# Cross-attention and graph layers on one core: router logits and low-rank activations computed row by row, and the router moved on VectorE

## The chip, the core and the metric

One core of a Trainium2 chip runs the whole program in one launch. The metric is the device time of that launch in microseconds. TensorE multiplies into PSUM, VectorE and ScalarE read PSUM, GpSimd works in SBUF only, and SyncE issues most DMAs. Each engine takes its own instructions in program order; they meet only through semaphores.

## What is computed

For 4 batches of 256 rows of 512 values (cut to what matters):

```python
# lora_A is ctx_4096 seen as (4, 64, 512); the kernel sums its 4 parts first
logits = x @ router_W.T + router_b            # (b, s, 8)
w      = softmax(logits)
a_sum  = einsum('bsh,arh->bsr', x, lora_A)    # (b, s, 64)
x1     = nan_to_num(x + 0.5 * sum_n w_n * (a_sum @ lora_B[n].T))
# 32 heads of cross-attention over 64 context rows, residual, layer norm
points = layernorm(x1 + attention(x1, ctx) @ Wo.T + bo) * g + b
# two graph layers of four blocks each; neighbours are the 8 nearest of 512 columns of ctx
for 8 blocks: p = leaky(points); points += (W_i @ (p + sum over 8 neighbours of p)) / 9
```

The diff touches the first four lines only. `a_sum` and the logits come out of one product with a matrix of 64 + 8 = 72 columns, `a_router`.

## The kernel before

The work on TensorE is cut into *uses* of PSUM. PSUM holds four slots of 1024 fp32 columns, and `tile_order()` writes out the order of all uses by hand, as (kind, batch, part). Use number n goes to slot n mod 4. Before TensorE starts use n, `wait_read` makes it wait until the reader of use n-4 is done (the table `read_by` says which semaphore and count that is); readers wait with `wait_full`. Every engine walks through the same list and does its own part of each kind, so the list is also the order of work on ScalarE, VectorE, GpSimd and SyncE.

The list has an opening for batch 0 (square, distance 0, lora_a, router, distance 1, keys, mixed, update, values, query). Then, for b = 0 to 2 with n = b+1, the attention of batch b is interleaved with the low-rank update and the neighbours of batch n: rows b, adjacency b, lora_a n, scores b 0 and 1, square n, router n, scores b 2 and 3, distance n 0, mixed n, shift b, update n, weights b, and so on. Batch 3's attention is interleaved with the first graph blocks, and the other graph blocks run in loops over two slots for W and two for the neighbour sums.

What the router does, kind by kind:

- **lora_a**: TensorE multiplies `a_router` (stationary, 72 columns) with `x_in` (moving, 256 columns), 4 chunks, so the result has 72 rows and one column per query (L538). ScalarE copies it to `low` (L746).
- **router**: TensorE turns `low` into two tiles of 128 queries by 72 columns with two transposes (L558). VectorE first waits for `q_lo` of the batch before (GpSimd's L913, since `mix` lies where `q_full` lay), then adds the bias (`lg`, L1168), takes the maximum and subtracts it (`lgs`, L1171). ScalarE takes the exponential (`lge`, L764). VectorE sums, inverts and multiplies (`lgw`, L1175) and writes `mix`, the low-rank activations times each of the 8 weights (L1177, two instructions).
- **mixed**: TensorE transposes `mix` (8 transposes, L572). ScalarE makes the high part `mixT_hi` (L773), VectorE the low part `mixT_lo` (L1187).
- **update**: TensorE multiplies with `lora_B` in three partial products (L576); it needs `mixT_lo`. VectorE adds the result to x and clamps it to `x1`.

Around it: **scores** (2 matmuls of 512 columns each, L593) are read by VectorE's four maxima (`shift`, L1243). **square** starts with ScalarE's `xyz_sq` (L758) and ends with its copy into `xyz_n` (L760). **distance** (2 fp32 products of 512 columns, L565, each recorded as two instructions) needs `xyz_n`; its reader is `nearest` on VectorE (L1034 to L1039), for part 0 of batches 1 to 3 only behind the shift. **adjacency** ends with ScalarE's copy to `adj` (L858). **shift** transposes the maxima (L598); SyncE sends them to `q_stack` (L443), and **weights** waits for that. From the second batch on, SyncE sends the inverted sums of the batch before (`inv_out`, L1049, made by VectorE behind the shift) ahead of it. GpSimd makes the next batch's `k_blk_hi` (L906) once scores 3 is done.

Of the kernel before, what the change touches and what calls it, by code (L numbers as in the profile page):

```python
# [17 lines left out]
ACT = mybir.ActivationFunctionType  # L18
# [30 lines left out]
def tile_order():  # L49

    order = [("square", 0, 0), ("distance", 0, 0), ("lora_a", 0, 0), ("router", 0, 0), ("distance", 0, 1),
             ("keys", 0, 0), ("mixed", 0, 0), ("update", 0, 0), ("values", 0, 0), ("query", 0, 0)]
    for b in range(B - 1):
        n = b + 1
        order += [("rows", b, 0), ("adjacency", b, 0), ("lora_a", n, 0), ("scores", b, 0), ("scores", b, 1),
                  ("square", n, 0), ("router", n, 0), ("scores", b, 2), ("scores", b, 3), ("distance", n, 0),
                  ("mixed", n, 0), ("shift", b, 0), ("update", n, 0), ("weights", b, 0), ("weights", b, 1)]
        order += [("output", b - 1, 0)] * (b > 0)
        order += [("weights", b, 2), ("distance", n, 1), ("attend", b, 0), ("weights", b, 3), ("query", n, 0),
                  ("attend", b, 1)]  # L60

    b = B - 1
    order += [("rows", b, 0), ("adjacency", b, 0)] + [("scores", b, i) for i in range(4)]
    order += [("wp", 0, 0), ("shift", b, 0), ("wp", 1, 0), ("spread", 0, 0), ("output", b - 1, 0),
              ("weights", b, 0), ("weights", b, 1), ("weights", b, 2), ("attend", b, 0), ("weights", b, 3),
              ("attend", b, 1), ("wp", 2, 0), ("spread", 1, 0), ("output", b, 0), ("spread", 2, 0),
              ("wp", 0, 1), ("wp", 3, 0), ("spread", 0, 1), ("wp", 1, 1), ("spread", 3, 0), ("wp", 2, 1),
              ("spread", 1, 1), ("wp", 3, 1), ("spread", 2, 1), ("spread", 3, 1)]
    return order


def xattn_graph_kernel(nc, xT, ctx, ctxT, mask, maskT, fsideT, lora_BT, router_WT, router_b,
# [9 lines left out]
    with stack:  # L82
# [5 lines left out]
        def sem(name):  # L88
            return stack.enter_context(nc.semaphore(name))
# [10 lines left out]
        def fb(name, shape, dt=F32):  # L100
            return sb(name, shape, dt, front)
# [19 lines left out]
        mixT_hi = fb("mixT_hi", [P, KC, S], F32R)  # L121
        low = fb("low", [R + NE, S])
        a_router = fb("a_router", [P, KC, R + NE])
# [91 lines left out]
        a_ready = sem("a_ready")  # L215
        low_ready = sem("low_ready")
        lgs_ready = sem("lgs_ready")
# [73 lines left out]
        def wait_full(eng, *key):  # L291
# [5 lines left out]
        read_by = {  # L297
            "lora_a": (low_ready, lambda b, i: b + 1), "keys": (k_ready, lambda b, i: KC),
            "values": (v_ready, lambda b, i: 1), "square": (norm_ready, lambda b, i: b + 1),
            "router": (mix_ready, lambda b, i: ST * (b + 1)), "distance": (near_ready, lambda b, i: KC * b + 2 * i + 2),  # L300
            "mixed": (mixT_lo_ready, lambda b, i: b + 1), "update": (raw_ready, lambda b, i: b + 1),
# [173 lines left out]
        def _(pe):  # L475
# [50 lines left out]
            for key in order:  # L526
# [5 lines left out]
                if kind == "lora_a":  # L532
                    loaded(pe, f"x{b}")
                    if b == 0:
                        pe.wait_ge(a_ready, 1)
                        loaded(pe, "routerW")
                    for k in range(KC):
                        last = mm(ps[0:R + NE, 0:S], a_router[:, k, :], x_in[:, k, :], k == 0, k == KC - 1)  # L538
                elif kind == "keys":
# [11 lines left out]
                elif kind == "square":  # L551
                    pe.wait_ge(sq_ready, b + 1)
                    pe.wait_ge(dve_consts, 2)
                    last = mm(ps[0:V + 1, 0:H], half_neg[:], xyz_sq[:], True, True)
                elif kind == "router":
                    pe.wait_ge(low_ready, b + 1)
                    for t in range(ST):
                        last = pe.transpose(ps[:, t * P:t * P + R + NE], low[:, t * P:(t + 1) * P],  # L558
                                            ident[0:R + NE, 0:R + NE])
                elif kind == "distance":  # L560
# [112 lines left out]
        def _(act):  # L673
# [64 lines left out]
            for key in order:  # L738
                kind, b, i = key
                ps = slot(key)  # L740
                if kind == "lora_a":
                    if b >= 1:

                        wait_full(act, "router", b - 1, 0)
                    wait_full(act, *key)
                    act.activation(low[:], ps[0:R + NE, 0:S], ACT.Copy).then_inc(low_ready, 1)  # L746
                elif kind == "keys":
# [5 lines left out]
                elif kind == "square":  # L753
# [6 lines left out]
                    act.activation(xyz_n[V:V + 1, :], ps[V:V + 1, 0:H], ACT.Copy).then_inc(norm_ready, 1)  # L760
                elif kind == "router":

                    act.wait_ge(lgs_ready, b + 1)
                    act.activation(lge[:], lgs[:], ACT.Exp).then_inc(lge_ready, 1)  # L764
                    if b == 0:
                        loaded(act, "loraB")
                        act.activation(flat(loraB_hi), flat(loraB_raw), ACT.Copy).then_inc(loraB_hi_ready, 1)
                elif kind == "mixed":
# [111 lines left out]
        def _(pool):  # L880
# [43 lines left out]
            for key in order:  # L924
                kind, b, i = key
                if kind == "router" and b == 0:
                    pool.wait_ge(loraB_hi_ready, 1)
# [50 lines left out]
        def _(dve):  # L978
# [166 lines left out]
            for key in order:  # L1145
# [5 lines left out]
                if kind == "values":  # L1151
# [4 lines left out]
                       .then_inc(v_ready, 1)  # L1156
                elif kind == "router":
                    loaded(dve, "rb")
# [213 lines left out]
```

## Time and profile before

| what | value |
|---|---|
| median of 3 runs | 461.76 us (461.59 to 470.96) |
| span of the profiled execution | 462.6 us |
| TensorE busy | 407.9 us, 88% |
| VectorE busy | 289.6 us, 63% |
| ScalarE busy | 157.7 us, 34% |
| GpSimd busy | 139.4 us, 30% |

All times in the profile are us from the span's first instruction. The first 264 us hold the attention, the rest the graph blocks. PE is TensorE's matmuls, PEld its weight loads, DVE VectorE, ACT ScalarE, POOL GpSimd, SPq the queue of SyncE. In a row of the timeline, "idle before <-releaser" is the time in which the engine had nothing to do ahead of that row, and what ended it. All matmuls are issued by one helper at L477, so they are told apart by the names behind the line: out <- moving, stationary. An fp32 product is recorded as two matmul instructions with two weight loads, a transpose as one.

### The profile page before, as it was taken

What the parts mean: (1) busy time and instruction counts of PE and PEld (TensorE: products, weight loads), DVE (VectorE), ACT (ScalarE), POOL (GpSimd) and SP (SyncE); (2) the same over time, 40 slices, a digit from 0 to 9 for tenths busy, and PEclk for the clock granted to TensorE, in tenths of its full rate; (3) what the DMA queues carried; (4) which work ended last, traced back from release to release, by engine and by line L of the source; (5) the groups of instructions that cost most, each with busy time, mean ns of one, the idle gap of its engine ahead of it and who ended that gap; (6) DMA issues with size and microseconds to landing.
All of it is one profiled execution on the core that took longest, in us unless ns stands there. A gap on an engine that the chain in (4) does not pass through costs nothing.

```text
span 462.6 us, 5745 instructions
## 1 busy us (share of the span) xinstructions
PE 407.9 (88%) x2216; PEld 333.7 (72%) x2216; DVE 289.6 (63%) x327; ACT 157.7 (34%) x193; POOL 139.4 (30%) x94
## 2 busy tenths in 40 slices
PE   5979297997899779968777989999999999999996
PEld 1566275784858475847365678898898888898894
DVE  1859828647783678596438764665656665665633
ACT  2230042364217522753182243223332224233310
POOL 2344723016003900190001223434424342344400
PEclk9999688999799979998989989999999999999999
DMA  6910434028120912013400000000000000000012
GB/s 202 408 63 0 150 77 110 14 94 162 31 68 8 186 40 91 4 44 85 99 3 25 1 0 1 0 2 0 0 0 1 1 0 0 0 0 0 0 75 107
DMA packets 22568, 24.90 MB, mean 54 GB/s; under 512 B 5508, under 2 KB 16756, under 8 KB 22548
## 3 DMA queue, kind: packets, MB, share of 16 engines
q1 hardware_dynamic: 21524, 23.44, 17.8%
q0 software_dynamic: 576, 1.18, 1.2%
q8 instruction: 13, 0.21, 0.2%
q10 hardware_dynamic: 448, 0.01, 0.1%
q14 instruction: 7, 0.06, 0.0%
HBM read 14.69 MB, written 3.38 MB: 39 GB/s over the span
## 4 chain that ended last, share of the span: by engine, by line
PE 68%; DMA 7%; DVE 6%; issue 6%; ACT 5%; SPq 4%; POOL 3%; DVEq 0%; ACTq 0%; POOLq 0%
PE slot L477 67%; DMA q_stack<-shiftT 3%; SPq L353 3%; DMA inv_bounce<-inv_out 2%; DMA sums_bounce<-sums 1%; ACT probT L813 1%; DVE shift L1243 1%; POOL points L921 1%; DVE p_lo L1122 1%; ACT attT L853 1%; POOL q_lo L913 1%; ACT sums L851 1%; DMA xyz_n<-in_ctx 1%; SPq L412 1%; DVE mix L1177 1%
## 5 line engine op out<-in xcount | busy, mean ns | idle before, releaser
L913 POOL TENSOR_TENSOR p_lo<-p_full,p_hi 128x1024 fp32r<-128x1024 f32 x29 | 69.5, 2398 | 160.8 <-ACT p_hi L688 160.8
L688 ACT ACTIVATE p_hi<-p_full 128x1024 fp32r<-128x1024 f32 x32 | 33.9, 1060 | 129.0 <-DVE p_full L997 128.9
L1086 DVE TENSOR_TENSOR u_lo<-slot,u_hi 128x1024 fp32r<-128x1024 f32 x32 | 38.8, 1222 | 49.6 <-ACT u_hi L729 49.6
L477 PE MATMUL slot<-adj,u_hi 128*128 128x512 f32 x256 | 64.8, 395 | 0.2
L477 PE MATMUL slot<-adj,u_lo 128*128 128x512 f32 x256 | 63.3, 389 | 0.0
L477 PE MATMUL slot<-fs_hi,p_hi 128*128 (+1 forms) x256 | 52.9, 289 | 7.5 <-DVE p_lo L1122 6.1
L1093 DVE SCALAR_TENSOR_TENSOR points<-slot,points 128x1024 f32<-128x1024 f32 x32 | 39.2, 1224 | 30.2 <-PE slot L477 30.2
L477 PEld LDWEIGHTS slot<-adj,u_lo 128*128 128x128 f32 x256 | 48.1, 188 | 10.0
L477 PEld LDWEIGHTS slot<-adj,u_hi 128*128 128x128 f32 x256 | 46.5, 188 | 10.3 <-issue 1.6
L477 PE MATMUL slot<-fs_lo,p_hi 128*128 (+1 forms) x256 | 52.8, 289 | 0.0
L477 PE MATMUL slot<-fs_hi,p_lo 128*128 (+1 forms) x256 | 52.7, 288 | 0.0
L477 PEld LDWEIGHTS slot<-fs_hi,p_hi 128*128 128x128 f32 x256 | 42.5, 197 | 10.5 <-issue 8.8
L997 DVE SCALAR_TENSOR_TENSOR p_full<-points 128x1024 f32<-128x1024 f32 x32 | 46.2, 1445 | 2.7
L477 PEld LDWEIGHTS slot<-fs_lo,p_hi 128*128 128x128 f32 x256 | 41.1, 198 | 0.0
L477 PEld LDWEIGHTS slot<-fs_hi,p_lo 128*128 128x128 f32 x256 | 41.0, 197 | 0.0
L729 ACT ACTIVATE u_hi<-slot 128x1024 fp32r<-128x1024 f32 x32 | 32.5, 1015 | 21.1 <-PE slot L477 20.4
L477 PE MATMUL slot<-probT,v_blk 128*128 128x256 f32 x128 | 30.8, 394 | 3.9 <-ACT probT L813 3.9
L477 PEld LDWEIGHTS slot<-probT,v_blk 128*128 128x128 f32 x128 | 24.9, 198 | 9.3 <-issue 3.1
L813 ACT ACTIVATE probT<-slot,mask_col 128x1024 f32<-128x1024 f32 x16 | 17.4, 1111 | 41.4 <-PE slot L477 41.3
L477 PE MATMUL slot<-wo,attT 128*128 128x512 f32 x64 | 28.3, 595 | 2.6 <-issue 2.6
L920 POOL TENSOR_TENSOR points<-points,g_all 128x1024 f32<-128x1024 f32 x2 | 4.7, 2356 | 66.4 <-DVE points L1080 66.4
L477 PEld LDWEIGHTS slot<-wo,attT 128*128 128x128 f32 x64 | 11.8, 190 | 16.8 <-issue 16.8
(138 smaller groups left out, 586.8 us busy)
## 6 DMA issues: line engine op xcount, KB each, us to landing
q_stack<-q_hi SPq DMA_DIRECT2D x32, 128.0 KB, 3.6
x_in<-in_xT SPq DMA_DIRECT2D x4, 512.0 KB, 4.0
q_stack<-q_lo SPq DMA_DIRECT2D x16, 128.0 KB, 4.5
out_points<-points SPq DMA_DIRECT2D x4, 512.0 KB, 2.8
inv_sums<-inv_bounce SPq DMA_DIRECT2D x7, 256.0 KB
loraB_raw<-in_lora_BT SPq DMA_DIRECT2D x1, 1024.0 KB, 9.4
wk<-in_WkT SPq DMA_DIRECT2D x1, 1024.0 KB, 11.5
wq_raw<-in_WqT SPq DMA_DIRECT2D x1, 1024.0 KB, 10.5
```

The source lines that it names most:

```text
L353: eng.dma_start(q_stack[PART * part:PART * (part + 1), j::HC // 2, :].bitcast(F32), q[PART * j:PART * (j + 1)].bitcast(F32))\
L412: sp.dma_start(inv_sums[:, 2 * i:2 * i + 2].rearrange("p c s -> p (c s)"), back.rearrange("g h n -> (g h) n").unsqueeze(1).broadcast_to([H ...
L477: return pe.matmul(dst, lhsT, rhs, start=start, stop=stop, skip_group_check=True)
L688: act.activation(p_hi[:, b, :], p_full[:, half, :], ACT.Copy).then_inc(p_hi_ready, 1)
L729: act.activation(u_hi[:, half].rearrange("p m o -> p (m o)"), ps[:], ACT.Copy)\
L813: act.activation(probT[:, i % 2, :], ps[:], ACT.Exp, bias=mask_col[:, b:b + 1], scale=QK_SCALE).then_inc(prob_ready, 1)
L851: act.activation(sums[V:2 * V, :], ps[V:2 * V, :], ACT.Copy).then_inc(att_read, 1)
L913: pool.tensor_tensor(lo, full, hi.bitcast(F32), ALU.subtract).then_inc(ready, 1)
L920: link(pool.tensor_tensor(pts, pts, g_all[:].unsqueeze(1).broadcast_to([P, ST, H]), ALU.mult))
L997: dve.scalar_tensor_tensor(p_full[:, half, :], pts, SLOPE, pts, ALU.mult, ALU.max)\
L1086: dve.tensor_tensor(u_lo[:, half].rearrange("p m o -> p (m o)"), ps[:], u_hi[:, half].rearrange("p m o -> p (m o)").bitcast(F32), ALU.subt ...
L1093: dve.scalar_tensor_tensor(pts, ps[:], 1.0 / (TOPK + 1), pts, ALU.mult, ALU.add)\
```

## The change

- `lora_a` swaps the operands: the 128 queries of a tile are now the stationary side and `a_router` the moving one. The result already has queries on rows, in the layout that the transposes gave. For each of 2 tiles 4 chunks are summed: 8 products of 72 columns instead of 4 of 256.
- The copy to `low`, the tile `low`, its semaphore and the two transposes go, and so does the use `router` of PSUM. The list is four uses shorter, and the slot distances of the uses near the former `router` change with it. The reader of a `lora_a` use is now VectorE's `mix`.
- What VectorE, ScalarE and GpSimd did at `router` they now do at `lora_a`. In batches 1 to 3 that is ahead of scores 0 and 1 on VectorE, and ahead of `xyz_sq` of the same batch on ScalarE.

```diff
-    order = [("square", 0, 0), ("distance", 0, 0), ("lora_a", 0, 0), ("router", 0, 0), ("distance", 0, 1),
+    order = [("square", 0, 0), ("distance", 0, 0), ("lora_a", 0, 0), ("distance", 0, 1),
...
         order += [("rows", b, 0), ("adjacency", b, 0), ("lora_a", n, 0), ("scores", b, 0), ("scores", b, 1),
-                  ("square", n, 0), ("router", n, 0), ("scores", b, 2), ("scores", b, 3), ("distance", n, 0),
+                  ("square", n, 0), ("scores", b, 2), ("scores", b, 3), ("distance", n, 0),
...
-            "lora_a": (low_ready, lambda b, i: b + 1), "keys": (k_ready, lambda b, i: KC),
+            "lora_a": (mix_ready, lambda b, i: ST * (b + 1)), "keys": (k_ready, lambda b, i: KC),
...
-                    for k in range(KC):
-                        last = mm(ps[0:R + NE, 0:S], a_router[:, k, :], x_in[:, k, :], k == 0, k == KC - 1)
+                    for t in range(ST):
+                        for k in range(KC):
+                            last = mm(ps[:, t * P:t * P + R + NE], x_in[:, k, t * P:(t + 1) * P],
+                                      a_router[:, k, :], k == 0, k == KC - 1)
...
-                elif kind == "router":
-                    pe.wait_ge(low_ready, b + 1)
-                    for t in range(ST):
-                        last = pe.transpose(ps[:, t * P:t * P + R + NE], low[:, t * P:(t + 1) * P],
-                                            ident[0:R + NE, 0:R + NE])
...
                 if kind == "lora_a":
-                    if b >= 1:
-
-                        wait_full(act, "router", b - 1, 0)
-                    wait_full(act, *key)
-                    act.activation(low[:], ps[0:R + NE, 0:S], ACT.Copy).then_inc(low_ready, 1)
+
+                    act.wait_ge(lgs_ready, b + 1)
+                    act.activation(lge[:], lgs[:], ACT.Exp).then_inc(lge_ready, 1)
+                    if b == 0:
+                        loaded(act, "loraB")
+                        act.activation(flat(loraB_hi), flat(loraB_raw), ACT.Copy).then_inc(loraB_hi_ready, 1)
...
-                if kind == "router" and b == 0:
+                if kind == "lora_a" and b == 0:
...
-                elif kind == "router":
+                elif kind == "lora_a":
                     loaded(dve, "rb")
                     if b >= 1:
```

What follows that last line is unchanged: `dve.wait_ge(q_lo_ready, b)`, the wait for the slot, and the router's instructions.

## Rows read from the trace of the kernel before

**Rows 1.** The profile's page: the chain that ended last, its shares by line.

```profile
PE slot L477 67%; DMA q_stack<-shiftT 3%; SPq L353 3%; DMA inv_bounce<-inv_out 2%; DMA sums_bounce<-sums 1%; ACT probT L813 1%; DVE shift L1243 1%; POOL points L921 1%; DVE p_lo L1122 1%; ACT attT L853 1%; POOL q_lo L913 1%; ACT sums L851 1%; DMA xyz_n<-in_ctx 1%; SPq L412 1%; DVE mix L1177 1%
```

**Rows 2.** The same chain in order of time: start, us, what.

```profile
268.50 63.48 PE slot L477 x384
```

**Rows 3.** Timeline, the opening: start us, us, instructions [idle before <-releaser].

```profile
11.26 3.62 PE L477 MATMUL slot<-x_in,a_router 128*72 128x256 f32 x8
...
15.35 0.50 PE L558 MATMUL slot<-ident,low 72*128 72x72 f32 x2 [0.47 <-ACT low L746]
15.64 3.71 PE L477 MATMUL slot<-xyz_n,xyz 65*128 65x512 f32 x4
...
19.15 9.01 PE L477 MATMUL slot<-ctx_t,wk 128*128 128x256 f32 x32
```

**Rows 4.** Timeline, stretch 1 (batch 1's router in batch 0's attention).

```profile
64.80 1.90 PE L477 MATMUL slot<-x_in,a_router 128*72 128x256 f32 x8
...
66.03 2.38 POOL L913 TENSOR_TENSOR q_lo<-q_full,q_hi 128x1024 fp32r<-128x1024 f32 x1 [10.69 <-ACT q_hi L791]
...
67.20 2.36 DVE L1243 TENSOR_REDUCE shift<-slot 128x16 f32<-128x1024 f32 x2 [1.80 <-PE slot L477]
...
69.57 0.34 PE L558 MATMUL slot<-ident,low 72*128 72x72 f32 x2
...
70.05 0.17 DVE L1168 TENSOR_TENSOR lg<-slot,rb_all 128x16 f32<-128x16 f32 x1 [0.50 <-PE slot L558]
...
70.67 0.22 ACT L764 ACTIVATE lge<-lgs 128x16 f32<-128x16 f32 x1 [0.41 <-DVE lgs L1171]
...
70.73 1.88 PE L477 MATMUL slot<-xyz_n,xyz 65*128 65x512 f32 x4
...
72.08 1.29 DVE L1177 TENSOR_TENSOR mix<-slot,lgw 128x512 f32<-128x512 f32 x2
...
73.52 1.07 PE L572 MATMUL slot<-ident,mix 128*128 128x128 f32 x8 [0.91 <-DVE mix L1177]
```

**Rows 5.** Single lines: duration ns min/median/max, first and last start us, forms.

```profile
L558 PE MATMUL slot<-ident,low x8: 226/282/382, 15.3 to 156.0; 72*128 72x72 f32 x8
...
L572 PE MATMUL slot<-ident,mix x8: 272/273/302, 73.5 to 74.3; 128*128 128x128 f32 x8
...
L1175 DVE TENSOR_TENSOR lgw<-lge,small x4: 175/720/817, 17.2 to 158.6; 128x16 f32<-128x16 f32 x4
```

**Rows 6.** Timeline, stretch 2 (batch 2's router in batch 1's attention).

```profile
105.06 1.88 ACT L858 ACTIVATE adj<-slot 128x2048 fp32r<-128x2048 bf16 x1
...
112.74 1.06 PE L572 MATMUL slot<-ident,mix 128*128 128x128 f32 x8 [0.91 <-DVE mix L1177]
...
116.66 0.55 DVE L1049 RECIPROCAL inv_out<-sums_in 64x64 f32<-64x64 f32 x1
...
125.45 1.19 PE L477 MATMUL slot<-q_stack,k_stack 100*128 100x256 f32 x8 [0.66 <-DMA q_stack<-shiftT]
```

**Rows 7.** Timeline, stretch 3 (batch 3's router in batch 2's attention).

```profile
152.20 1.88 ACT L858 ACTIVATE adj<-slot 128x2048 fp32r<-128x2048 bf16 x1
...
156.64 1.28 ACT L764 ACT_TABLE_LOAD   x1
...
160.87 1.06 PE L572 MATMUL slot<-ident,mix 128*128 128x128 f32 x8 [1.91 <-DVE mix L1177]
...
162.03 1.02 ACT L773 ACTIVATE mixT_hi<-slot 128x1024 fp32r<-128x1024 f32 x1 [3.88 <-PE slot L572]
...
163.53 1.23 DVE L1187 TENSOR_TENSOR mixT_lo<-slot,mixT_hi 128x1024 fp32r<-128x1024 f32 x1 [0.54 <-DMA sums_bounce<-sums]
...
165.48 0.55 DVE L1049 RECIPROCAL inv_out<-sums_in 64x64 f32<-64x64 f32 x1 [0.28 <-DMA sums_in<-sums_bounce]
```

**Rows 8.** Windows: us, PE, PEld, DVE, ACT, POOL busy, PEclk, DMA share, GB/s.

```profile
67.00:77.00 10.00, 6.08 (x25) 2.92 (x23) 8.72 (x14) 4.11 (x9) 5.45 (x5) 1.00 0.69 159
78.00:81.00 3.00, 3.00 (x16) 3.00 (x16) 2.90 (x7) 0.00 (x0) 0.00 (x0) 0.50 0.08 22
```

More of the change, by code:

```diff
@@ L121, in xattn_graph_kernel @@
         mixT_hi = fb("mixT_hi", [P, KC, S], F32R)
-        low = fb("low", [R + NE, S])
         a_router = fb("a_router", [P, KC, R + NE])
@@ L215, in xattn_graph_kernel @@
         a_ready = sem("a_ready")
-        low_ready = sem("low_ready")
         lgs_ready = sem("lgs_ready")
@@ L297, in xattn_graph_kernel @@
         read_by = {
-            "lora_a": (low_ready, lambda b, i: b + 1), "keys": (k_ready, lambda b, i: KC),
+            "lora_a": (mix_ready, lambda b, i: ST * (b + 1)), "keys": (k_ready, lambda b, i: KC),
             "values": (v_ready, lambda b, i: 1), "square": (norm_ready, lambda b, i: b + 1),
-            "router": (mix_ready, lambda b, i: ST * (b + 1)), "distance": (near_ready, lambda b, i: KC * b + 2 * i + 2),
+            "distance": (near_ready, lambda b, i: KC * b + 2 * i + 2),
             "mixed": (mixT_lo_ready, lambda b, i: b + 1), "update": (raw_ready, lambda b, i: b + 1),
@@ L760, in _ @@
                     act.activation(xyz_n[V:V + 1, :], ps[V:V + 1, 0:H], ACT.Copy).then_inc(norm_ready, 1)
-                elif kind == "router":
[L763 to L767, printed above, removed]
                 elif kind == "mixed":
@@ L1156, in _ @@
                        .then_inc(v_ready, 1)
-                elif kind == "router":
+                elif kind == "lora_a":
                     loaded(dve, "rb")
```

## The prediction

> **What bounds the kernel now.** I read the chain of waits first. By line, TensorE's helper holds two thirds of it and no single wait holds more than 3% [rows 1]. From 268.5 us on the chain in order of time is one row of matmuls after another (the first is shown) [rows 2], none of them touched by the change, so whatever the change does happens before that, where the chain changes engine every few microseconds. The timeline of those stretches shows four places: the opening (batch 0's router), and the three places where batch n's router runs inside batch n-1's attention; I call these stretch 1, 2 and 3, after n.
>
> In the opening TensorE is busy nearly without a break from 11.3 to 28.2 us and waits 0.47 us for `low` [rows 3]. In stretch 1 (64 to 79 us) the chain is: maxima, router, `mix`, the `mixed` transposes, `mixT_hi`, `mixT_lo`, `update`. TensorE is busy 6.1 of 10 us there, VectorE 8.7 [rows 8]: VectorE and its order set the pace, and TensorE waits 0.91 us for `mix` before L572 [rows 4]. In stretch 2 the same order holds, and behind `mixT_lo` come the reciprocal of the sums and, in SyncE's order, three DMAs; the `weights` matmuls wait 0.66 us for the last, the shift stack [rows 6]. In stretch 3 `mixT_lo` and the reciprocal themselves wait a little for DMAs (0.54 and 0.28 us) [rows 7].
>
> **The change, part by part.**
>
> *1. The lora_a matmuls.* Before: 4 fp32 products of 256 columns, each two instructions, so 8: 3.62 us in the opening [rows 3], 1.90 us in stretch 1 [rows 4]. The same eight instructions are 0.43 and 0.21 us apart, 4 and 2 cycles of 2.4 GHz per column, so the opening runs at the 1.2 GHz level although the clock records there say nothing. Now: 2 x 4 products of 72 columns, so 16 instructions of 72 columns on 128-column weights. No row has this form. The nearest are the two transposes of L558: 128 columns of weights, 72 moving, fp32. Two take 0.34 us where one takes 0.28, so they stand 0.06 us apart [rows 4, 5], and 0.50 against 0.38, 0.12 apart, at the low clock [rows 3, 5]. From above I bound them by the fp32 transposes with 128 columns moving, L572: eight take 1.07 us where one takes 0.27, so 0.11 apart [rows 4, 5]; 0.21 at the low clock. So 16 cost 0.96 to 1.8 us at the high clock and 1.9 to 3.4 us in the opening. Only two in a row were seen at 0.06, so I go by the middle. The Trainium skill, "TensorE: Matmul & The Clock Gate", section "LDWEIGHTS (loading the stationary operand)", says that a weight load costs its number of columns divided by 1.2, in ns, whatever the rows: 107 ns here. The two transposes 0.06 us apart don't agree, if what they show holds for more than two. By the rule the opening's 16 would take 1.9 us, since the low clock's spacing is already above 0.107, and the sum below would come out 0.4 us lower; in stretches 1 to 3 it changes nothing, because those matmuls end before what gates the router.
>
> *2. The copy and the transposes.* ScalarE's `low` (between the adjacency copy and `xyz_sq`) and two transposes go. In stretches 1 to 3 both lie beside VectorE's maxima and cost nothing now. In the opening they are on TensorE's path: the second distance tile stood behind them and started at 15.64.
>
> *Opening, sum.* Start of lora_a 11.26 plus 1.9 to 3.4 gives a second distance tile at 13.2 to 14.7 instead of 15.64: `keys` (19.15) starts 0.9 to 2.5 us earlier [rows 3]. `keys` has 32 instructions, the first ones at 0.43, the last at 0.21 (9.01 us in all). If TensorE's clock rises at the same moment as now, a microsecond won on the low side of it does the work of half a microsecond on the high side: 0.5 to 1.2 us at the end of `keys`. The rest of the opening (k copies, `mixT`, `update`, VectorE's long row of masks and clamps up to `x1`) hangs on that and moves with it. I take **-0.85 us**.
>
> *3. VectorE's router goes ahead of maxima 0 and 1.* The order becomes rows, router, maxima 0 to 3. Two things follow.
>
> (a) What gates the router. At its head stands the wait for `q_lo` of the batch before, since `mix` lies over `q_full`. Before, that was long done. Now in stretch 1 it is not: GpSimd makes `q_lo` from 66.03 to 68.41 [rows 4]. VectorE, which before began its maxima at 67.20, stands until 68.45 with all four maxima behind it. In stretch 2 `q_lo` is done in time, and the exp waits for ScalarE's adjacency copy (105.06 + 1.88 = 106.94) [rows 6]. In stretch 3 that copy ends at 154.08 and the exp table's load of 1.28 us follows, 155.36 [rows 7].
>
> (b) PSUM slots. Each use waits until the use four places before it has been read. With the router's use gone, scores 2 waits for `mix` (before: maximum 0), scores 3 for maximum 0, and the first distance tile for **maximum 1** (before: only for a ScalarE copy). The distance tile takes 1.88 us on TensorE, and `mixed` is queued behind it. Before, it ran at 70.73, hidden under the router [rows 4]; now it runs after maximum 1, on the path from `mix` to `mixed`.
>
> *Stretch 1.* lg starts 68.45. From lg to `mix` takes 72.08 - 70.05 = 2.03 us, of which lgw takes 0.72; it took 0.175 at least [rows 4, 5], in the opening, when GpSimd was idle. GpSimd's key blocks now start only after scores 3, so I take 0.175: 1.49 us. `mix` 69.94 to 71.23; maxima 0 and 1 (2.36 together) to 73.55; semaphore to TensorE 0.15; distance tile 73.70, its four matmuls 4 x 0.427 = 1.71 to 75.41; `mixed` 75.41 against 73.52 [rows 4]. All behind it keeps its distances (the maxima 2 and 3 end at about 75.9, before they are wanted): **+1.9 us**. TensorE is without a break from there to the end of `attend`, so this is paid in full.
>
> *Stretch 2.* Exp 106.98. In stretch 1 it starts 70.67 - 70.05 = 0.62 after lg [rows 4], and `mix` would start 1.49 - 0.62 = 0.87 after it: `mix` 107.87 to 109.16; maximum 1 ends 111.5; distance tile 111.65; `mixed` 113.36 against 112.74: **+0.6 us**, which goes through the reciprocal at 116.66 and its DMAs to `weights` at 125.45 [rows 6].
>
> *Stretch 3.* Exp 155.42; `mix` 156.3 to 157.6; maximum 1 159.9; `mixed` 161.79 against 160.87. Before, `mixT_lo` waited for a DMA until 163.53; now `mixT_hi` is done at 161.79 + 1.16 + 1.02 = 163.97, and `mixT_lo` starts 164.0; the reciprocal moves from 165.48 to 165.75 [rows 7]: **+0.3 us**. If lgw kept its 0.72, each stretch would lose 0.55 more.
>
> SyncE and GpSimd issue the same DMAs in the same order; none is added.
>
> *Sum.* -0.85 + 1.9 + 0.6 + 0.3 = **+1.95 us**, with bounds -1.2 + 2.8 = +1.6 and -0.5 + 2.8 + 1.65 = +3.95 (lgw slow in all three). The profiled execution has a span of 462.6 us and the median of the runs shown is 461.76, 0.8 lower; I add the difference to the median: 463.7 us.
>
> **Rivals.**
>
> *A. TensorE's clock falls sooner.* It fell behind stretch 1: after 6.1 us busy of 10 it was at the 1.2 GHz level (0.50) from 78 to 81 us [rows 8]. Now TensorE has a gap at 67.6 to 70 and only three short pieces until 73.7. If it falls before the distance tile, that tile (1.71) and `mixed` (0.87) take double, +2.6 us, on the path. Once: 466.3 us. In all three stretches: 463.7 + 7.8 = 471.5 us, over 2% slower. It decides only if the clock falls before about 73.7 us in stretch 1 and likewise in the others. Against it: it stayed at full rate through 67 to 77 as things are.
>
> *B. The opening wins more.* With no break between lora_a and the distance tile, the clock may rise before `keys`. Then 32 x 0.213 = 6.8 us from about 17.5 ends at 24.3 instead of 28.16, 3.9 us instead of 0.85: 460.7 us. For it: TensorE is denser there. Against: it was nearly as dense from 11.3 to 19 and stayed low.
>
> *C. Nothing moves.* The router's four copies and eight transposes were hidden, and the new waits fall into slack such as stretch 2's 0.66 us. Then only the opening counts, or not even that: 461 to 462 us. Against: in stretch 1 there is no slack between `mixT_lo` and `update`.
>
> **Chances.** The forecast (462.7 to 465.5) 0.58; A in one stretch 0.15 (466.3), A in all 0.04 (471.5); B 0.14 (460.7); C 0.09 (461.5). The range leaves out A in all and the tails of B and A: 460.5 to 467.0. About 2%, 9.2 us, is what a measurement of this kernel can tell from no change: over 2% slower only in A in all, 0.04; over 2% faster in none of the cases, 0.01 left for what I don't see; same 0.95.
>
> **What would show it.** Sixteen lora_a instructions taking 1.0 to 2.0 us in stretch 1. VectorE idle until about 68.4 in stretch 1, released by GpSimd's `q_lo`. The distance matmuls behind a wait for a maximum (L1243), and `mixed` directly behind them with no wait for `mix`. `mixed` 1.9, 0.6 and 0.9 us later than before, relative to each stretch's first score matmul. lgw at 0.18 us. `keys` 0.9 to 2.5 us earlier. I am wrong if `q_lo` doesn't hold the router, if the distance tile isn't held by maximum 1, or if the clock records differ from before by more than one low stretch.

## The result and the profile after

| | before | after |
|---|---|---|
| median of the comparison, us | 466.36 (461.59 to 471.23, 4 runs) | 476.28 (474.18 to 479.18, 4 runs) |
| ratio | | 1.0323, 95% interval 1.0274 to 1.0372 |
| span of the profiled execution, us | 462.6 | 474.9 |
| mean granted clock of TensorE, share of full | 0.956 | 0.929 |

The changed kernel is 3.2% slower. The ratios here leave out slow runs, of the kernel before two of the four (470.96 and 471.23 us), so the 3.2% are not the 2.1% that the two medians give. Forecast was 463.7 us, 460.5 to 467.0.

The opening after, TensorE's timeline (start us, us, instructions):

```profile
11.32 3.53 PE L475 MATMUL slot<-a_router,x_in 128*128 128x72 f32 x16
14.64 3.71 PE L475 MATMUL slot<-xyz_n,xyz 65*128 65x512 f32 x4
18.15 8.94 PE L475 MATMUL slot<-ctx_t,wk 128*128 128x256 f32 x32
26.93 1.04 PE L567 MATMUL slot<-ident,mix 128*128 128x128 f32 x8
```

`keys` starts 1.0 us earlier than in [rows 3], and `mixed` of batch 0, at 26.93, starts 1.1 us earlier than in that trace (28.00). Sixteen lora_a instructions take 3.53 us; one alone takes 0.42, so they stand (3.53 - 0.42)/15 = 0.21 us apart. In stretch 1 they take 1.96, 0.11 apart. Both spacings are the upper bounds of the prediction, and the totals lie a little above its 3.4 and 1.8 us.

Stretch 1 after, the timeline of all engines:

```profile
61.92 1.03 PE L580 MATMUL slot<-ident,x 128*128 128x128 f32 x8
...
63.69 1.96 PE L475 MATMUL slot<-a_router,x_in 128*128 128x72 f32 x16
...
64.92 2.37 POOL L902 TENSOR_TENSOR q_lo<-q_full,q_hi 128x1024 fp32r<-128x1024 f32 x1 [10.65 <-ACT q_hi L780]
...
67.81 0.17 DVE L1157 TENSOR_TENSOR lg<-slot,rb_all 128x16 f32<-128x16 f32 x1 [3.52 <-POOL q_lo L902]
...
69.08 0.18 DVE L1164 TENSOR_TENSOR lgw<-lge,small 128x16 f32<-128x16 f32 x1
...
69.27 1.51 PE L475 MATMUL slot<-xyz_sq,half_neg 64*65 64x512 f32 x2 [2.65 <-issue]
69.30 1.29 DVE L1166 TENSOR_TENSOR mix<-slot,lgw 128x512 f32<-128x512 f32 x2
70.50 4.61 DVE L1232 TENSOR_REDUCE shift<-slot 128x16 f32<-128x1024 f32 x4
...
72.90 0.50 PEld L475 LDWEIGHTS slot<-xyz_n,xyz 65*128 65x128 f32 x2 [0.63 <-DVE shift L1232]
72.90 3.78 PE L475 MATMUL slot<-xyz_n,xyz 65*128 65x512 f32 x4
...
76.48 1.92 PE L567 MATMUL slot<-ident,mix 128*128 128x128 f32 x8
...
80.87 1.20 PE L475 MATMUL slot<-mixT_hi,loraB_hi 128*128 128x256 f32 x4 [2.05 <-issue]
```

Each wait that the prediction named for stretch 1 is there. VectorE stands 3.52 us for GpSimd's `q_lo`; the distance tile is released by a maximum (L1232); `mixed` follows it directly; lgw takes 0.18. But the tile takes 3.78 us where it took 1.88 in [rows 4], and `mixed` 1.92 instead of 1.07: TensorE is at its 1.2 GHz level. Windows of the kernel after (us, PE, PEld, DVE, ACT, POOL busy, PEclk, DMA share, GB/s):

```profile
67.00:70.00 3.00, 0.73 (x2) 0.19 (x2) 1.74 (x8) 0.73 (x2) 0.29 (x1) 0.95 0.89 204
70.00:77.00 7.00, 7.00 (x12) 2.93 (x12) 5.11 (x5) 0.59 (x1) 3.92 (x4) 0.50 0.53 123
77.00:86.00 9.00, 6.95 (x33) 6.43 (x32) 5.85 (x10) 2.40 (x6) 0.12 (x1) 0.50 0.03 7
109.00:120.00 11.00, 8.71 (x47) 5.19 (x44) 7.59 (x13) 4.78 (x7) 7.72 (x11) 1.00 0.86 169
165.00:178.00 13.00, 10.54 (x33) 6.96 (x32) 8.44 (x12) 2.40 (x6) 4.04 (x4) 0.51 0.34 63
```

TensorE did 0.73 us of work in the 3 us before 70, then had half the clock (0.50) from 70 to 86, where [rows 8] show 1.00 up to 77. In stretch 3 the clock was down over the tile and `mixed` too (0.51 from 165 to 178 us). In stretch 2 the clock stayed up (1.00), and there the waits can be read alone:

```profile
116.40 1.98 PE L475 MATMUL slot<-xyz_n,xyz 65*128 65x512 f32 x4 [0.41 <-DVE shift L1232]
118.22 1.04 PE L567 MATMUL slot<-ident,mix 128*128 128x128 f32 x8
...
130.74 1.71 PE L475 MATMUL slot<-q_stack,k_stack 100*128 100x256 f32 x8 [3.07 <-DMA q_stack<-shiftT]
```

TensorE waits 3.07 us for the shift stack, against 0.66 in [rows 6]: at the full clock `update` took 5.9 us (121.7 to 127.7) instead of 8.5 (116.3 to 124.8), and the DMA was no earlier for it.

Where the time went, by the starts of the transposes of x (`rows`, one per batch), in us. Each row is one profiled execution, so the same code differs by what the clock did. Most are not the median execution: e2, e5, e7 and e12 were traced at their highest time, e3, e15 and e17 at their lowest or within 0.2 us of it.

| kernel | rows 0 | to rows 1 | to rows 2 | to rows 3 | rest of the span | span |
|---|---|---|---|---|---|---|
| before | 63.0 | 39.5 | 47.1 | 48.6 | 264.3 | 462.6 |
| before, second trace (e17) | 58.7 | 39.5 | 47.2 | 48.8 | 263.3 | 457.5 |
| after | 61.9 | 45.5 | 49.2 | 53.7 | 264.7 | 474.9 |
| e1, new form, old place | 63.1 | 40.9 | 52.4 | 54.0 | 264.1 | 474.5 |
| e2, old form, new order | 58.4 | 44.5 | 54.7 | 51.5 | 264.3 | 473.4 |
| e3, late q_lo wait | 61.6 | 40.7 | 49.6 | 53.7 | 264.8 | 470.4 |
| e5, after, filled | 63.5 | 40.3 | 49.0 | 52.0 | 263.7 | 468.5 |
| e6, before, filled | 60.4 | 39.7 | 47.2 | 50.6 | 263.9 | 461.7 |
| e7, after, filled more | 61.9 | 43.0 | 47.2 | 52.0 | 264.2 | 468.3 |
| e12, tile behind and late wait | 63.7 | 40.0 | 49.4 | 51.4 | 264.9 | 469.4 |
| e10, before with the new opening | 61.5 | 40.5 | 49.0 | 53.9 | 264.6 | 469.4 |
| e15, e10 with a warm-up | 61.5 | 39.5 | 47.2 | 48.7 | 263.1 | 459.9 |

Against the first trace of before the change loses 6.0, 2.0 and 5.1 us in the three stretches, and wins 1.1 in the opening.

### The profile page after: what moved, and what is told of

Same layout as the page of the kernel before. It is cut to its first block, busy times and chain, and to the rows that moved or that the text cites. A ratio compares the mean times of both kernels' runs of the same rounds, so it can differ in the third digit from the quotient of the medians.

```text
span 474.9 us, 5783 instructions
## 1 busy us (share of the span) xinstructions
PE 416.7 (88%) x2240; PEld 339.8 (72%) x2240; DVE 288.2 (61%) x327; ACT 156.2 (33%) x189; POOL 139.6 (29%) x94
## 4 chain that ended last, share of the span: by engine, by line
PE 76%; issue 7%; DVE 5%; ACT 5%; DMA 4%; POOL 3%; SPq 0%; DVEq 0%; ACTq 0%; POOLq 0%
PE slot L475 74%; DMA q_stack<-shiftT 2%; DVE shift L1232 1%; ACT probT L802 1%; PE slot L567 1%; DMA inv_bounce<-inv_out 1%; POOL points L910 1%; DVE p_lo L1111 1%; ACT attT L842 1%; POOL q_lo L902 1%; ACT sums L840 1%; DMA xyz_n<-in_ctx 1%; POOL points L909 0%; DVE p_full L986 0%; POOL p_lo L902 0%
## 5 line engine op out<-in xcount | busy, mean ns | idle before, releaser
L1075 DVE TENSOR_TENSOR u_lo<-slot,u_hi 128x1024 fp32r<-128x1024 f32 x32 | 38.9, 1225 | 49.4 <-ACT u_hi L724 49.4
L475 PE MATMUL slot<-wo,attT 128*128 128x512 f32 x64 | 32.7, 670 | 3.6 <-issue 3.6
L475 PE MATMUL slot<-probT,v_blk 128*128 128x256 f32 x128 | 29.4, 381 | 3.9 <-ACT probT L802 3.9
L475 PEld LDWEIGHTS slot<-probT,v_blk 128*128 128x128 f32 x128 | 23.8, 190 | 9.0 <-ACT probT L802 3.0
L475 PEld LDWEIGHTS slot<-wo,attT 128*128 128x128 f32 x64 | 13.6, 219 | 20.6 <-issue 20.6
```

The source lines that it names most:

```text
L475: return pe.matmul(dst, lhsT, rhs, start=start, stop=stop, skip_group_check=True)
L1075: dve.tensor_tensor(u_lo[:, half].rearrange("p m o -> p (m o)"), ps[:], u_hi[:, half].rearrange("p m o -> p (m o)").bitcast(F32), ALU.subt ...
```

## The experiments

All ratios are to runs of the kernel before on the same chip. The kernels that fill TensorE's idle time add matmuls whose results nobody reads; e17 is the kernel before.

**e1: the router in its old place, with the new form.**

```diff
-        order += [("rows", b, 0), ("adjacency", b, 0), ("lora_a", n, 0), ("scores", b, 0), ("scores", b, 1),
-                  ("square", n, 0), ("scores", b, 2), ("scores", b, 3), ("distance", n, 0),
+        order += [("rows", b, 0), ("adjacency", b, 0), ("scores", b, 0), ("scores", b, 1),
+                  ("square", n, 0), ("lora_a", n, 0), ("scores", b, 2), ("scores", b, 3), ("distance", n, 0),
```

> The changed kernel, but in batches 1 to 3 the new lora_a (queries on rows, no copy, no transposes) stands where the router stood before, behind maxima 0 and 1 and the square; the PSUM distances there are then those of before. If the order and the slots make the loss (theory): the wait for q_lo and the distance tile behind maximum 1 are gone, mixed starts as in before or a little earlier, and with the opening's 0.9 to 1.1 us the span is 460 to 463 us. If the swapped operands themselves are slower or lower TensorE's clock (rival): it stays within 3 us of the changed kernel, 471 to 477 us.

Measured: 475.66 us, ratio 1.0295 (1.0213 to 1.0377). The forecast missed, and not for the rival's reason alone. Stretch 1 of e1:

```profile
69.39 2.00 PE L475 MATMUL slot<-a_router,x_in 128*128 128x72 f32 x16
...
71.53 0.17 DVE L1157 TENSOR_TENSOR lg<-slot,rb_all 128x16 f32<-128x16 f32 x1 [2.29 <-PE slot L475]
...
74.99 1.06 PE L567 MATMUL slot<-ident,mix 128*128 128x128 f32 x8 [0.90 <-DVE mix L1166]
```

The old place had 0.34 us of transposes between the maxima and the router, with the matmuls done earlier beside them; now 2.0 us of matmuls stand there and VectorE waits 2.29 us. I had moved the matmuls into the path, so e1 neither clears the order of the charge nor shows the new form to be slow by itself. That wait put `mixed` 1.4 us later behind `rows` (11.87 us, before 10.48); stretch 1 as a whole lost 1.4 us. Most of the loss is in stretches 2 and 3 (5.3 and 5.4 us); in stretch 2 the clock was down from 110 to 121 us (0.53).

**e2: the old form, the new order.** In the kernel before, `("router", n, 0)` moves directly behind `("lora_a", n, 0)`.

> The kernel before with its old matmuls, copy and transposes, but the router use moved directly behind lora_a, so that VectorE takes the router ahead of maxima 0 and 1 and the slots are waited for as in the changed kernel. Theory (order and slots): slow like the changed kernel, span 470 to 480 us, with mixed behind the distance tile and the clock at the 1.2 GHz level during them in stretch 1. Rival (swapped operands): like the kernel before, 461 to 465 us.

Measured: 473.31 us, ratio 1.0212 (1.0106 to 1.0317). Order and slots alone give most of the loss, with copy, transposes and old operands in place. Its profiled execution had the low clock from about 68.2 to 75.1 us, across `mixed` of stretch 1 (73.06).

**e3: the q_lo wait at the writing of mix.**

```diff
-                        dve.wait_ge(q_lo_ready, b)
...
+                    if b >= 1:
+                        dve.wait_ge(q_lo_ready, b)
                     for t in range(ST):
                         dve.tensor_tensor(mix[:, t], tiles[:, t, 0:R].unsqueeze(1).broadcast_to([P, NE, R]),
```

> The changed kernel with the wait for q_lo moved from the router's head to just before mix is written, the only tile that lies over q_full. In stretch 1 the logits and the exp then run while GpSimd makes q_lo, and mix starts at about 67.5 us instead of 69.3, so mixed 1.8 us earlier. If the q_lo wait is one part of the loss and only that: 1.8 us less, 472 to 473 us. If it also opens the gap in which TensorE's clock falls: the clock stays up through the distance tile and mixed in stretch 1, another 2.7 us, 469 to 471 us.

Measured: 473.26 us, ratio 1.0287 (1.0192 to 1.0383). In its profiled execution stretch 1 fell from 45.5 to 40.7 us, `mixed` at 11.7 us behind `rows` instead of 14.6, and the clock stayed up through it, as the second theory had it; but stretch 3 was as slow as before the edit (53.7). The median is 3 us below the changed kernel's; the intervals of the two ratios overlap, so the wait's own share is not settled.

**e5: the changed kernel, filled.**

```diff
                 elif kind == "square":
+                    if b >= 1:
+                        for _ in range(10):
+                            mm(ps[:, H:2 * H], x1_hi[:, 0, 0:P], wq_hi[:, 0, :], True, True)
                     pe.wait_ge(sq_ready, b + 1)
...
                 elif kind == "update":
+                    if b >= 1:
+                        for _ in range(8):
+                            mm(ps[:, 0:H], x1_hi[:, 0, 0:P], wq_hi[:, 0, :], True, True)
                     pe.wait_ge(mixT_lo_ready, b + 1)
```

> The changed kernel with idle TensorE time filled in batches 1 to 3: ten extra matmuls of 512 columns (about 2.1 us) before the square's wait and eight (1.7 us) before update's, written to unused or later overwritten columns. They add TensorE work only. Theory (the low clock stretches at 69.5 to 86.5 and 165 to 178.7 us make 6 to 8 of the 12.3 us): the clock stays up there, and the span falls by 5 to 8 us to 467 to 470 us, though the fill costs up to 1 us. Rival (the waits alone make the loss): no change or slower, 475 to 479 us.

Measured: 468.88 us, ratio 1.0136 (1.0054 to 1.0217). Fifty-four extra matmuls make the changed kernel about 7 us faster. Stretch 1 of e5, TensorE's timeline:

```profile
63.48 1.03 PE L586 MATMUL slot<-ident,x 128*128 128x128 f32 x8
...
74.49 1.99 PE L475 MATMUL slot<-xyz_n,xyz 65*128 65x512 f32 x4 [0.40 <-DVE shift L1238]
76.31 1.04 PE L570 MATMUL slot<-ident,mix 128*128 128x128 f32 x8
```

The clock stayed at 1.00 from 69.5 to 86.5 us here, and the tile is back to 1.99 us. `mixed` starts 12.83 us behind `rows`, against 10.48 in before and 14.56 in after: of the 4.1 us that stretch 1 loses up to there, 2.35 are waits and 1.7 clock.

**e6 and e7: both orders filled.** e6 is the kernel before with 4 such matmuls before the square, 4 before `update`, and 10 before the weights' wait for the shift stack; e7 is the changed kernel with 10, 8 and 12.

> The kernel before with idle TensorE time filled in batches 1 to 3 by extra matmuls of 512 columns whose results nobody reads: 4 before the square's wait, 4 before update's, and 10 before the weights' wait for the shift stack (batches 1 and 2). This gives the old order a reference in which the clock stays up. If the low stretches are what makes its runs differ (459 to 471 us), its low stretches between 64 and 210 us are gone and it is as fast as the best runs before or a little faster, 458 to 462 us. If filling costs more than it saves: 463 to 467 us.

> The changed kernel with 10 such matmuls before the square's wait, 8 before update's and 12 before the weights' wait. With the clock up in both, the difference to the filled kernel before is the waits alone. Theory (waits +2.8 us as worked out in the prediction, opening -1.1 us, the rest of the loss is clock): 1 to 3 us above the filled kernel before, 460 to 465 us, with no low stretch between 64 and 190 us. Rival (waits or the operand swap make more than 5 us): 467 us or more.

Measured: e6 462.50 us, ratio 0.9979 (0.9937 to 1.0020); e7 467.01 us, ratio 1.0102 (1.0033 to 1.0171). Filled, the two orders are 4.5 us or 1.2% apart (1.0102/0.9979); as they were, 9.9 us by the medians and 3.2% by the ratio. So more than half of the loss goes when TensorE is kept busy. The 4.5 us are more than the 1 to 3 expected for the waits. They are no clean figure for the waits either, since the fill did not keep the clock up everywhere: e6 was still at 0.50 from 73.5 to 76.8 and from 158.9 to 162.2 us, and e7's windows show

```profile
66.00:73.00 7.00, 5.76 (x20) 2.83 (x18) 4.69 (x11) 1.95 (x4) 1.70 (x2) 1.00 0.72 166
73.00:80.00 7.00, 7.00 (x18) 4.47 (x19) 2.57 (x3) 1.47 (x3) 3.66 (x4) 0.51 0.28 63
```

TensorE was busy 5.8 of 7 us and the clock fell all the same, just before the tile. In e7's stretch 2, where it didn't, the two filled kernels take 47.2 us both.

**e8, e9: the waits taken out of the filled kernel.** e8 adds e3's edit. e9 adds the distance tile behind `mixed`:

```diff
-                  ("square", n, 0), ("scores", b, 2), ("scores", b, 3), ("distance", n, 0),
-                  ("mixed", n, 0), ("shift", b, 0), ("update", n, 0), ("weights", b, 0), ("weights", b, 1)]
+                  ("square", n, 0), ("scores", b, 2), ("scores", b, 3), ("mixed", n, 0),
+                  ("distance", n, 0), ("shift", b, 0), ("update", n, 0), ("weights", b, 0), ("weights", b, 1)]
```

> The filled changed kernel with the wait for q_lo moved to just before mix is written (4 fill matmuls before the square instead of 10, since that gap is smaller then). If the q_lo wait is 1.2 to 1.8 us of stretch 1's 1.9: 1 to 2 us less than e7. If it is hidden: the same as e7.

> As e8, and the first distance tile goes behind mixed in TensorE's order, so that mixed stands directly behind scores 3 and waits for maximum 1 only. If the distance tile in front of mixed is the other part of the waits (1.7 us of TensorE per stretch): mixed starts 1.7 us earlier in each stretch; 1.7 us are won in stretch 1, less in 2 and 3, where a DMA and the maxima 2 and 3 end later: 2 to 4 us less than e8. If the shift behind it then ends last: no change.

Measured: e8 468.37 us, ratio 1.0151 (1.0077 to 1.0224); e9 463.69 us, ratio 1.0010 (0.9964 to 1.0056). The late wait gained nothing there, but e8's fill before the square was also smaller (4 matmuls for 10). From e8 to e9 the median falls by 4.7 us; e9 has 4 fill matmuls before `update` where e8 has 8, so the tile's move is not the only difference. e18, below, has the move alone.

**e12, e18: the same without fill.** e12 is the changed kernel with both edits, e18 with the tile's alone.

> The changed kernel with the distance tile behind mixed and the late wait for q_lo, without any fill. The waits found so far then are gone (mixed 9 to 10 us after the rows transposes, instead of 14.6 in the changed kernel). If the waits also made the low clock: 462 to 465 us, all of the loss is back. If the clock falls all the same, since the maxima still keep TensorE idle: 466 to 472 us.

> The changed kernel with only the first distance tile moved behind mixed. The late q_lo wait alone gave 3 us (e3), both together 9 us (e12). If the tile is the larger part: 4 to 7 us below the changed kernel, 469 to 472 us. If it works only together with the q_lo wait: 474 to 476 us.

Measured: e12 467.21 us, ratio 1.0058 (1.0009 to 1.0106); e18 468.52 us, ratio 1.0128 (1.0044 to 1.0211). One change in the list of uses takes the loss from 3.2% to 1.3%. In e12's stretch 1 the order is what the edit wants, at a low clock:

```profile
71.42 2.27 PE L475 MATMUL slot<-k_blk_hi,q_hi 128*128 128x512 f32 x4
73.60 1.97 PE L567 MATMUL slot<-ident,mix 128*128 128x128 f32 x8
75.36 3.62 PE L475 MATMUL slot<-xyz_n,xyz 65*128 65x512 f32 x4
```

`mixed` starts 9.9 us behind `rows`, earlier than in before (10.5), and the tile's doubled time no longer stands in front of it.

**e10, e11: the opening alone, and all but the opening.** e10 is the kernel before with the new form in batch 0 only, e11 the changed kernel with the old form there.

> The kernel before with the new lora_a form in batch 0 only; batches 1 to 3 are as before. By the prediction's opening term: 0.5 to 1.2 us faster, 462 to 464 us where before gives 463 to 465. Rival, from the eight openings traced so far (with the old form TensorE reached 2.4 GHz at about 14 and 15.5 us in two of three, with the new form before 19 us in none of seven): short matmuls with 72 columns keep the clock down longer, the row of keys matmuls starts at the low clock and ends 1 to 3 us later than in those, and the kernel is 0 to 3 us slower than before, 464 to 468 us.

> The changed kernel with the old lora_a, copy and transposes in batch 0 only. By the opening term: 0.5 to 1.2 us slower than the changed kernel, 476 to 478 us. Rival as in e10: 0 to 3 us faster, 473 to 476 us.

Measured: e10 470.93 us, ratio 1.0137 (1.0069 to 1.0204); e11 474.46 us, ratio 1.0228 (1.0173 to 1.0283). The opening was to win 0.85 us; alone it loses 6 in e10's median. The second trace of before (e17) shows what the first one had hidden:

```profile
11.26 3.60 PE L477 MATMUL slot<-x_in,a_router 128*72 128x256 f32 x8
...
15.52 1.93 PE L477 MATMUL slot<-xyz_n,xyz 65*128 65x512 f32 x4
17.28 7.07 PE L477 MATMUL slot<-ctx_t,wk 128*128 128x256 f32 x32
24.19 1.04 PE L572 MATMUL slot<-ident,mix 128*128 128x128 f32 x8
```

The second distance tile takes 1.93 us and `keys` 7.07, not 3.71 and 9.01 as in [rows 3]: here TensorE reached the 2.4 GHz level by the end of lora_a. Over all profiled executions `mixed` of batch 0 started, with the old form, at 28.0 (the first trace), 23.8, 24.2, 23.7, 24.1, 24.0, 24.2 and 24.0 us (before, e2, e6, e11, e14, e16, e17, e19); with the new form at 26.0 to 27.9 us in all twelve, and in each of these the second distance tile took 3.7 us. So the new form keeps TensorE at 1.2 GHz past lora_a and the tile, and costs some 3 us at `mixed` against seven of eight executions of the old one.

**e14, e15: the opening warmed.** Eight bf16 matmuls of 512 columns go into idle time ahead of lora_a, into the kernel before (e14) and into e10 (e15).

```diff
                 elif kind == "square":
+                    if b == 0:
+                        for _ in range(5):
+                            mm(ps[:, H:2 * H], ident_h, ident_wide[:, 0:H], True, True)
...
                 elif kind == "distance":
+                    if (b, i) == (0, 0):
+                        for _ in range(3):
+                            mm(ps[:, 0:H], ident_h, ident_wide[:, 0:H], True, True)
```

> The kernel before with eight extra bf16 matmuls of 512 columns in the opening's idle time on TensorE (5 before the first square's wait, 3 before the first distance's), results overwritten or never read. If the clock rises before lora_a (11.3 us) the lora_a, distance and keys matmuls run at 2.4 GHz and mixed starts at 20 to 23 us instead of 23.7 to 28: 1 to 4 us less than before, 460 to 463 us. If the warm-up doesn't raise it: no change.

> e10 (new form in batch 0 only) with the same eight matmuls. Clock theory: the clock is up before lora_a in both, the new form then saves the copy and the transposes, mixed starts 0.3 to 1 us earlier than in e14, and the time is within 1 us of e14 or below, 459 to 463 us. Rival (something else in the form costs 6 us): 5 us or more above e14, 465 to 469 us.

Measured: e14 464.68 us, ratio 1.0034 (0.9992 to 1.0075); e15 466.91 us (461.44 to 470.08), ratio 1.0016 (0.9956 to 1.0076). The warm-up did not do its work: the clock rose no earlier (`mixed` at 24.1 in e14, 26.7 in e15), so the pair doesn't test what it was made for. It shows the opening's 2.6 us at `mixed` once more. In the whole time it shows no loss clear of the noise: the medians are 2.2 us apart, and the ratio of e15, with the new opening, is no higher than e14's. And e15 is e10 but for the eight matmuls; both traces reach `rows` 0 at 61.5 us, and from there on the code is the same. Yet e10's takes 9.5 us longer (on another chip, but the kernel before has 464.65 us there and 464.75 here). One window of each (e10, then e15), with the clock as its last value but two:

```profile
125.00:129.00 4.00, 3.95 (x11) 2.43 (x12) 3.86 (x5) 2.12 (x2) 0.00 (x0) 0.57 0.00 0
```

```profile
125.00:129.00 4.00, 4.00 (x11) 1.81 (x10) 3.86 (x5) 1.81 (x2) 0.00 (x0) 1.00 0.00 0
```

So neither the code of a stretch nor the time at which it starts fixes where the clock is low. e10's 6 us can't be put down to the opening's own 3.

**e13, e16: candidates.** e13 is e12 with 4 fill matmuls before the square and 12 before the weights; e16 is the kernel before with e6's fill and e14's warm-up.

> e12 with fill: 4 matmuls before the square and 12 before the weights' wait, none before update, where the distance tile now fills the gap (in e9 tile and fill together made update start 7.0 us after mixed in stretch 1 instead of 3.5). Expected 1 to 3 us less than e9: 460 to 463 us, the first version that would beat the kernel before.

> The kernel before with both the warm opening of e14 and the fill of e6. If both gains add: 457 to 461 us, the first version below the kernel before by more than its interval. If fill gains nothing beyond the warm opening: like e14.

Measured: e13 465.28 us, ratio 1.0022 (0.9978 to 1.0067), above the 460 to 463 expected; e16 461.98 us, ratio 0.9953 (0.9909 to 0.9998). e16 is the fastest kernel of the study, below before by 0.5% with an interval that just leaves out 1; no version of the new order beats the kernel before.

**e17, e19.** The kernel before again; and the changed kernel with tile behind, late wait and the old opening.

> The kernel before, unchanged, for a second trace. If the low clock stretches differ from run to run by chance, they lie elsewhere than in the first trace (77.8 to 81.2, 115.4 to 122.2, 163.2 to 170.0 us) and the time is anywhere in 459 to 471 us; if the order of the work sets them, they lie within 3.5 us of those.

> The changed kernel with the tile behind mixed, the late q_lo wait, and the old lora_a form in the opening (so the new form and the new order stay in batches 1 to 3). If the three are the whole loss: like the kernel before, 461 to 466 us, and at least 2 us below e12, since mixed of batch 0 starts at 24 us instead of 27. If the new form costs in batches 1 to 3 too: 466 us or more.

Measured: e17 462.66 us (459.19 to 471.04, 10 runs); its low clock stretches in stretches 1 to 3 begin at 72.7, 110.2 and 158.0 us, each about 5 us earlier than in the first trace, so the 3.5 us that were to speak for the order of the work are missed. But the work is earlier too, by 4.3 us (`rows` 0 at 58.74 and 63.04), so against the work they moved by less than 1 us. Here order and clock went together; e10 and e15 show that they need not. e19: 465.82 us, ratio 1.0061 (1.0011 to 1.0112). `mixed` of batch 0 started at 24.0 us as hoped, but the median is only 1.4 us below e12's, not 2, and the ratio is no better (1.0061 against 1.0058).

## Why the prediction was wrong

*The waits: right, and near in size.* At the full clock `mixed` starts later behind `rows` by 2.35 us in stretch 1 (e5; predicted 1.9), 10.77 - 10.21 = 0.56 in stretch 2 (after; 0.6) and 12.02 - 11.21 = 0.8 in stretch 3 (e5; 0.9). The router was held by `q_lo`, the tile by maximum 1, lgw took 0.18, the exp in stretch 3 waited for the table load. The error in stretch 1 is mostly the router's start, 5.9 us behind `rows` where I had put 5.4: VectorE started 0.5 us behind the end of `q_lo` (64.92 + 2.37 = 67.29, `lg` at 67.81), and I had allowed 0.04.

*The step that failed first: rival A's weight.* A had the mechanism: the clock falls before the tile, and tile and `mixed` take double. It was given 0.04 for all stretches and 0.15 for one, on the ground that the clock had stayed at 1.00 from 67 to 77 us [rows 8]. That row was taken with 6.1 us of work in those 10; the change takes TensorE's work out of the first part of that time, and from 67 to 70 TensorE worked 0.73 us instead of 2.03. The clock was down over the tile in stretches 1 and 3. The sum had no term for it. The price of 2.6 us per stretch was also short, since it stopped at `mixed`: the low clock went on into `update`, to about 86.8 us, and stretch 1 lost 6.0 us, not 1.9 or 4.5. That the clock carries much of the loss is shown by e5 and by e6 against e7, where extra work makes the kernel faster.

*The second: the opening, with the wrong sign at `mixed`.* "If TensorE's clock rises at the same moment as now": it doesn't. The change moves that moment. The first trace of before was the odd one of eight, in which the old form had no advantage, and the prediction read a gain of 1.1 us from it that the one comparison of traces, 28.0 against 26.9, even seems to confirm. Against the other seven it is a loss of 3 us there. What the opening costs in the whole time stays open. e10's profiled execution loses 2.7 us to e17's up to `rows` 0, then 1.0, 1.8 and 5.1 us in stretches whose code is the same, with the clock low in other places; e15 lost nothing in them. With the old opening e11 is 1.8 us below the changed kernel by the medians and 1.0% by the ratios, and e19 by its ratio gains nothing on e12.

*The third: slack in front of a DMA is no slack for the clock.* Rival C took TensorE's wait for the shift stack as a place where time vanishes, and the forecast carried 0.6 us through it; neither asked at what clock TensorE would run ahead of the wait and behind it. In before `update` (116.3 to 124.8 us) ran at the low clock until about 122, and only 0.66 us of idling was left. In after `update` ran at full speed, TensorE then idled 3.07 us, and the clock was at 0.50 from 131.2 to 134.5 us, with the path on TensorE. Behind the wait, in before and in after:

```profile
126.47 7.03 PE L477 MATMUL slot<-wo,attT 128*128 128x512 f32 x16
```

```profile
132.25 8.18 PE L475 MATMUL slot<-wo,attT 128*128 128x512 f32 x16
```

The same 16 instructions take 1.15 us more (in e5 8.73, 1.7 more), and the `weights` matmuls ahead of them 1.71 instead of 1.19. What `update` had won at the full clock did not shorten the stretch, and this makes most of stretch 2's 2.0 us: `weights` itself starts only 23.3 us behind `rows` in after, instead of 22.9. In the filled kernels, where TensorE also worked ahead of that wait, the clock stayed up there, and stretch 2 took 47.2 us. That the idling made the clock fall is argued from this, not shown alone: e6 and e7 were filled in other places too.

*The band.* The band of 462.7 to 465.5 us does not come out of the sum either: its bounds, +1.6 and +3.95 on 461.76, give 463.4 to 465.7. The measured 476.28 us is outside both.

*The lora_a price.* I took the middle between 0.06 and 0.11 us per instruction; it is 0.11, and 0.21 at the low clock. Two transposes 0.06 us apart were no rate. The Trainium skill's rule ("TensorE: Matmul & The Clock Gate", "LDWEIGHTS (loading the stationary operand)", columns / 1.2 = 107 ns) was right at the full clock, where the trace's 0.112 agrees. At the low clock the trace's 0.207 does not: the spacing nearly doubled there.

*The split.* By the ratios, order and slots with the old form give 2.1% (e2), the tile's place about 1.9% of the 3.2% (after against e18), the opening's form 1.4% by itself (e10) but nothing in e15. They don't add up; that each acts mostly through the same clock fits the traces, and no run separates it. What the swapped operands cost by themselves in batches 1 to 3 was not run alone either. e19 has them there with the old opening, the tile behind `mixed` and the late wait, and is 0.6% slower than before.

## What to carry to other kernels

An edit that saves instructions on an engine with idle time can cost more than it saves, if the engine's clock falls when it is left idle, as it did here in stretch 1: before pricing the waits, ask how much TensorE still does in the microseconds ahead of each piece that will be on the path, and give the low clock a chance of its own there. When a slot or an order changes, look at what is queued in front of the critical instruction in its engine, not at that instruction's wait alone; here moving one tile behind `mixed` took back over half of the loss. And one trace is one draw: where durations of one instruction form differ by two inside it, get a second trace before pricing by the first.

## What the runs showed of the hardware

- The kernel before, unchanged, runs from 459 to 472 us over all comparisons, with the mean granted clock between 0.942 and 0.959; part of it is whether TensorE reaches 2.4 GHz at about 15 us or after 19: its two traces differ by 5.1 us of span, 4.3 of them ahead of `rows` 0. No execution of it above 465 us was traced.
- In the opening, the sixteen new lora_a instructions (3.5 us in a row) were followed by a second distance tile at the low clock in twelve executions of twelve, the eight old ones (2.9 to 3.6 us in the same place) by one at the full clock in seven of eight. TensorE's busy time in the profile is nearly the same for both (7.00 of the 7 us from 8 to 15 in after, 6.86 in e17).
- Eight bf16 matmuls of 512 columns ahead of them (3.8 us of TensorE time between 2.8 and 8.4 us) did not raise it earlier. They multiply an identity by a mostly empty matrix; whether data of full size would have is not tried.
- The clock fell at 73 us in e7 although TensorE had been busy 5.8 of the 7 us before.
- With the same code and `rows` 0 at 61.5 us in both, e10 had a low stretch at 125.6 to 129.0 us and e15 had none there; their spans are 469.4 and 459.9 us.
